# Row sums of the softmax: block sums on DVE for some tiles, turned sums on TensorE removed, two more split tiles per half

## The chip, the cores and the metric

The kernel runs on 1 core of one Trainium2 chip. The metric is the device time in microseconds of one execution; below, the median of three runs. The engines are TensorE (PE; its weight loads are shown as PEld), VectorE (DVE), ScalarE (ACT), GpSimd (POOL) and SyncE (SP), which here only issues DMAs.

## The reference, cut to what matters

A decoder layer on x [4, 256, 512] with a context of [4, 1601, 512], all in fp32:

```python
x = layernorm(x + self_attention(x))            # attention over head channels, 16 x 16 per token
x = layernorm(x + cross_attention(x, ctx))      # 32 query heads, 8 key heads of 128; keys are [ctx, x], 1857 rows
x = layernorm(x + router_mix(x))                # softmax over 64 experts, top 8

# cross attention, per batch and key head
q, k = rms_norm(x @ Wq) * qw, rms_norm(kv @ Wk) * kw
v = kv @ Wv
probs = softmax(q @ k.T / sqrt(128))            # the row sums of exp(...) are what the change is about
out = (probs @ v) @ Wo
```

## The kernel before, in words

Nearly all the time is cross attention. It is cut into 32 **units** (4 batches x 8 key heads), each of two **halves** of 2 query heads (512 columns: 2 heads x 256 queries), 64 halves in all. A half walks over 15 key **tiles** of 128 keys (the last has 65). Scores are kept transposed: keys on the partitions, the 512 query columns in the free dimension. The softmax's row sum is therefore a sum over partitions and tiles.

The whole order of work is written out by hand as numbered **steps**: step s computes the scores of tile s (`scores`), and ACT copies them into a ring of 21 rows in SBUF (`copy_scores`). DVE keeps the running maximum (`raise_max(s - 1)`); `scores(s)` waits for the maximum of tile s - 2, since there are two score banks. 18 steps later (WAIT), when the half's maximum is known, DVE shifts tile t = s - 18 (`shift`), ACT takes the exponential (`exp`), POOL does its part, and 2 steps after that PE multiplies with the values (`pv`).

Products in fp32 accuracy are done as three matmuls of split numbers (hi and lo parts, type fp32r): `three`. For the value product there are two ways. A **split** tile has P_hi from a second exponential on ACT (line 1322), P_lo from a subtraction on POOL (`lo`, line 888), and three matmuls (lines 971 to 973). A **full** tile is one fp32 product (line 1001), issued as two instructions; it needs neither. `FULL` lists the full tiles of a half per batch: 7, 5, 3 and 3 of 15. P_hi and P_lo have three buffers.

The row sums: POOL adds tile after tile into `acc` (`add`, lines 902 and 906, 14 adds per half). Then PE turns `acc` with four transposes (`turn_sums`, job "AT"), DVE reduces them to `sums` and takes the reciprocal `rinv` (lines 1726 and 1728), PE turns that again (`turn_reciprocals`, job "RT", line 1140), DVE copies it to `rrow` (line 1748), SP stores it to DRAM and loads it back spread over all partitions, and DVE multiplies the half's output `OT_n` with it (`divide`, line 1811). ACT and DVE split the result (`OT_hi`, `OT_lo`), and PE multiplies with Wo (jobs "O").

Beside this, PE does the next unit's projections: `fill(s)` gives a step's extra jobs by unit v and step c of its cycle of 30 (s = 30 v - 20 + c): "KV" (keys and values of a tile, at each even c), "Q", "QT" and "KT" (turned queries and keys), "X" (a tile of the context turned and split, via the buffers `built`), "MT" (turned maximum), "AT", "RT", "O". DVE drains a job in the step after it (`drain`), and normalises the queries at c = 13 (`normalise`, line 1675). The later tiles of the self attention (`LATER`) are products on POOL at the steps in `EVENTS`, with sums on DVE; the router of batch b runs beside a later batch. In the first batch POOL also splits the weights (`split`). Each engine's queue is in order, and each wait is on a semaphore's count.

The last unit has no next unit whose projections could run beside it: in its steps PE has scores, value products and outputs alone, and the last 20 steps have no scores either.

Of the kernel before, what the change touches and what calls it, by code (L numbers as in the profile page):

```python
# [45 lines left out]
def layer(nc, x_in, sWq, sbq, sWk, sbk, sWv, sbv, ctx_in, Wq, Wk, Wv, Wo, qw, kw, x1, y_out, Wr, rb, eb, final):  # L46
# [25 lines left out]
    FULL = [[2, 3, 6, 7, 10, 11, 14], [4, 5, 10, 11, 14], [6, 7, 14], [6, 7, 14]]  # L72
    FULL = [FULL[v // KVH] for v in range(UNITS)]
    HALF = [[j for j in range(NJ) if j not in FULL[v]] for v in range(UNITS)]
# [75 lines left out]
    def fill(s):  # L150
# [5 lines left out]
        if c % 2 == 0:  # L156
# [9 lines left out]
            12: [("RT", 2 * v - 3)],  # L166
# [9 lines left out]
            27: [("RT", 2 * v - 2), ("QT", v, 1)],  # L176
# [14 lines left out]
    def divided(s):  # L191
        return [x[1] for x in fill(s - 6) if x[0] == "RT"]
# [118 lines left out]
    def left(kind, v, at):  # L311
        return NJ * (2 * v - 3) + max(kind[v - 2][at]) + 1 if kind[v - 2][at] else 0

    with ExitStack() as ctx:
# [86 lines left out]
        built = [sb(f"built{i}", [P, 2, C, P], F32R) for i in range(2)]  # L401
# [3 lines left out]
        sums = sb("sums", [P, 2, 4])  # L405
        rinv = sb("rinv", [P, 2, 4])
        rrow = sb("rrow", [4, P])
# [113 lines left out]
        s_ri = sem("row_reciprocal")  # L521
# [76 lines left out]
        def _(e):  # L598
# [182 lines left out]
            for s in STEPS:  # L781
# [60 lines left out]
        def _(e):  # L842
# [48 lines left out]
            def add(t):  # L891
                p, j = divmod(t, NJ)
                if j == 0:
                    return
# [10 lines left out]
                e.wait_ge(s_acc, acc_no(t - 1))  # L905
# [60 lines left out]
        def _(e):  # L966
            e.wait_ge(s_id, 2)
            e.wait_ge(s_pad, 5)
# [222 lines left out]
            for s in STEPS:  # L1191
# [8 lines left out]
                for x in fill(s):  # L1200
# [12 lines left out]
                    elif x[0] == "AT":  # L1213
                        turn_sums(x[1])
# [10 lines left out]
                    elif x[0] == "RT":  # L1225
                        turn_reciprocals(x[1])
# [9 lines left out]
        def _(e):  # L1236
# [7 lines left out]
            e.wait_ge(s_pad, 5)  # L1244
# [44 lines left out]
            def copy_scores(s):  # L1289
# [11 lines left out]
                if s >= RING:  # L1301
# [6 lines left out]
                    e.wait_ge(s_acc, acc_no(t + 1 if t % NJ == 0 else t))  # L1308
# [43 lines left out]
            def high(job):  # L1352
                out = F_ps[F_AT[job] % 2][:]
                e.wait_ge(s_ff, F_AT[job] + 1)
                if job[0] == "X":
# [4 lines left out]
                    else:  # L1360
# [137 lines left out]
        def _(e):  # L1498
# [4 lines left out]
            e.wait_ge(s_pad, 5)  # L1503
# [190 lines left out]
            def drain(job):  # L1694
# [5 lines left out]
                if job[0] == "X":  # L1700
# [23 lines left out]
                elif job[0] == "AT":  # L1724
                    p = job[1]
                    e.reduce_sum(sums[:, p % 2, :], out.rearrange("p (i k) -> p i k", k=P), AX.X).then_inc(s_fr, 1)
                    e.wait_ge(s_fr, F_AT[job] + 1)
                    e.reciprocal(rinv[:, p % 2, :], sums[:, p % 2, :]).then_inc(s_ri, 1)
# [14 lines left out]
                elif job[0] == "RT":  # L1743
                    p = job[1]
                    if p:

                        e.wait_ge(s_rd, 16 * p)
                    e.tensor_copy(rrow[:], out[0:4, 0:P]).then_inc(s_fr, 1)
# [58 lines left out]

            def divide(p):
# [9 lines left out]
            for s in STEPS:  # L1818
# [69 lines left out]
```

## Time and profile before

| what | value |
|---|---|
| median of 3 runs | 2815.78 us (2813.55 to 2817.94) |
| profiled execution, own time | 2816.99 us |
| its span, first to last instruction | 2815.2 us |
| mean granted TensorE clock | 0.986 of 2.4 GHz |
| DMA | 485.6 MB, mean 173 GB/s |

Times in the profile are microseconds from the span's start, lengths of one instruction nanoseconds where marked. A PE matmul is drawn from its start to a modelled end, so that bars of neighbours overlap; DVE and ACT instructions overlap by up to some 0.1 us too. "[0.32 <-ACT ...]" behind a row is the engine's idle time before it and what ended it.

### The profile page before, as it was taken

How to read it: one execution, taken by the hardware profiler on the slowest of the kernel's cores; microseconds unless marked ns; L12 is line 12 of the kernel's file. 1: busy time of each engine (PE TensorE's matmuls, PEld its weight loads, DVE VectorE, ACT ScalarE, POOL GpSimd, SP SyncE). 2: the span in 40 equal slices, each digit the busy share in tenths (PEclk: the TensorE clock that was granted, in tenths of full speed). 3: DMA queues.
4: the chain of work that ended last, by engine and by line, in shares of the span. 5: the costliest groups of instructions: out<-in, count | busy, mean ns of one | idle time of the engine just before them, and what ended most of it. 6: DMA issues, size and time to landing. Idle time of an engine off the chain costs nothing.

```text
span 2815.2 us, 47816 instructions
## 1 busy us (share of the span) xinstructions
PE 2720.3 (97%) x14812; PEld 2220.4 (79%) x14812; DVE 2221.7 (79%) x3596; ACT 2029.4 (72%) x3945; POOL 2377.3 (84%) x2320
## 2 busy tenths in 40 slices
PE   7899999999999999999999999999999999999974
PEld 5777878777878888888888888888888888888853
DVE  5577888888778878888778887787778888788873
ACT  3577777777767777777777777777777777777771
POOL 4399999898888888878889988888898888888893
PEclk9999999999999999999999999999999999999996
DMA  6756565565555454555545455554455445344310
GB/s 234 253 184 216 193 221 193 195 213 184 183 178 200 160 177 169 182 177 196 178 147 193 167 189 174 179 184 165 156 173 173 154 158 180 124 165 150 117 42 26
DMA packets 159434, 485.64 MB, mean 173 GB/s; under 512 B 16839, under 2 KB 27849, under 8 KB 159182
## 3 DMA queue, kind: packets, MB, share of 16 engines
q1 hardware_dynamic: 157592, 481.01, 50.5%
q8 instruction: 121, 1.98, 0.3%
q10 hardware_dynamic: 1590, 1.58, 0.2%
q14 instruction: 131, 1.07, 0.1%
HBM read 403.09 MB, written 79.43 MB: 171 GB/s over the span
## 4 chain that ended last, share of the span: by engine, by line
PE 79%; POOL 9%; issue 6%; DVE 4%; ACT 2%; DMA 1%; SPq 0%; POOLq 0%; ACTq 0%; DVEq 0%
PE K_ps L971 9%; PE K_ps L973 9%; PE K_ps L972 9%; PE OT_ps L1001 7%; PE S_ps L971 6%; PE S_ps L973 6%; PE S_ps L972 6%; POOL acc L906 5%; PE OT_ps L971 5%; PE OT_ps L972 4%; PE OT_ps L973 4%; POOL P_lo L888 2%; PE F_ps L971 2%; PE F_ps L972 2%; PE F_ps L973 2%
## 5 line engine op out<-in xcount | busy, mean ns | idle before, releaser
L906 POOL TENSOR_TENSOR acc<-acc,scores 128x512 f32<-128x512 f32 (+1 forms) x832 | 1120.8, 1347 | 40.4 <-ACT scores L1323 10.1
L888 POOL TENSOR_TENSOR P_lo<-scores,P_hi 128x512 fp32r<-128x512 f32 x672 | 898.4, 1337 | 211.3 <-ACT scores L1323 210.3
L1652 DVE SCALAR_TENSOR_TENSOR running_max<-S_ps,rk,running_max 128x512 f32<-128x512 f32 (+1 forms) x896 | 669.0, 747 | 250.2 <-ACT scores L1309 247.8
L1636 DVE TENSOR_TENSOR scores<-scores,Mb_ps 128x512 f32<-128x512 f32 (+1 forms) x960 | 648.7, 676 | 134.4 <-PE Mb_ps L1127 134.3
L1309 ACT ACTIVATE scores<-S_ps,rk 128x512 f32<-128x512 f32 (+1 forms) x960 | 651.6, 679 | 139.8 <-PE S_ps L973 120.1
L1323 ACT ACTIVATE scores<-scores 128x512 f32<-128x512 f32 (+1 forms) x960 | 596.9, 622 | 59.2 <-DVE scores L1636 57.1
L1322 ACT ACTIVATE P_hi<-scores 128x512 fp32r<-128x512 f32 x672 | 423.1, 630 | 293.7 <-DVE scores L1636 213.9
L971 PE MATMUL S_ps<-QT_hi,KT_hi 128*128 128x512 f32 (+1 forms) x960 | 496.9, 518 | 14.8 <-DVE running_max L1652 13.0
L971 PE MATMUL K_ps<-Wkv_hi,kvT 128*128 128x256 f32 (+1 forms) x1664 | 470.9, 283 | 2.4 <-DVE kvT L1709 2.4
L973 PE MATMUL K_ps<-Wkv_hi,kvT 128*128 128x256 f32 (+1 forms) x1664 | 471.1, 283 | 0.0
L972 PE MATMUL K_ps<-Wkv_lo,kvT 128*128 128x256 f32 (+1 forms) x1664 | 470.3, 283 | 0.0
L973 PE MATMUL S_ps<-QT_hi,KT_lo 128*128 128x512 f32 (+1 forms) x960 | 380.6, 396 | 0.0
L972 PE MATMUL S_ps<-QT_lo,KT_hi 128*128 128x512 f32 (+1 forms) x960 | 379.3, 395 | 0.0
L971 PEld LDWEIGHTS K_ps<-Wkv_hi,kvT 128*128 128x128 f32 (+1 forms) x1664 | 310.3, 186 | 22.4 <-DVE kvT L1709 2.8
L972 PEld LDWEIGHTS K_ps<-Wkv_lo,kvT 128*128 128x128 f32 (+1 forms) x1664 | 310.3, 186 | 20.1
L971 PE MATMUL OT_ps<-P_hi,V_hi 128*128 128x512 f32 x672 | 290.3, 432 | 31.0 <-POOL P_lo L888 30.8
L973 PEld LDWEIGHTS K_ps<-Wkv_hi,kvT 128*128 128x128 f32 (+1 forms) x1664 | 310.7, 187 | 0.0
L1001 PE MATMUL OT_ps<-scores,V_full 128*128 128x512 f32 (+1 forms) x576 | 296.7, 597 | 0.0
L971 PEld LDWEIGHTS S_ps<-QT_hi,KT_hi 128*128 128x128 f32 (+1 forms) x960 | 178.1, 186 | 119.3 <-DVE running_max L1652 46.5
L972 PE MATMUL OT_ps<-P_lo,V_hi 128*128 128x512 f32 x672 | 266.6, 397 | 0.0
L973 PE MATMUL OT_ps<-P_hi,V_lo 128*128 128x512 f32 x672 | 266.0, 396 | 0.0
L972 PEld LDWEIGHTS S_ps<-QT_lo,KT_hi 128*128 128x128 f32 (+1 forms) x960 | 178.9, 186 | 92.4 <-issue 64.1
(226 smaller groups left out, 4666.8 us busy)
## 6 DMA issues: line engine op xcount, KB each, us to landing
kvT<-kvT_scratch SPq DMA_DIRECT2D x403, 512.0 KB, 3.7
Wq_hi<-weight_halves_scratch SPq DMA_DIRECT2D x48, 512.0 KB, 5.4
Wq_lo<-weight_halves_scratch SPq DMA_DIRECT2D x48, 512.0 KB, 6.6
Wo_hi<-weight_halves_scratch SPq DMA_DIRECT2D x48, 512.0 KB, 4.7
Wo_lo<-weight_halves_scratch SPq DMA_DIRECT2D x48, 512.0 KB, 5.6
kvT_scratch<-built SPq DMA_DIRECT2D x45, 512.0 KB, 4.3
rinv_spread<-rinv_scratch SPq DMA_DIRECT2D x64, 256.0 KB, 4.8
Wkv_hi<-weight_halves_scratch SPq DMA_DIRECT2D x24, 512.0 KB, 5.6
```

The source lines that it names most:

```text
L888: e.tensor_tensor(P_lo[n % PB][0:r, :], prob(t)[0:r, :], f(P_hi[n % PB][0:r, :]), ALU.subtract)\
L906: e.tensor_tensor(a[0:r, :], a[0:r, :], prob(t)[0:r, :], ALU.add).then_inc(s_acc, 1)
L971: e.matmul(out, l_hi, r_hi, start=first, stop=False)
L972: e.matmul(out, l_hi, r_lo, start=False, stop=False)
L973: return e.matmul(out, l_lo, r_hi, start=False, stop=last)
L1001: ins = e.matmul(OT_ps[:], V_full[v % 2][0:r, FULL[v].index(j), :], row[t % RING][0:r, :], start=first, stop=last)
L1309: e.activation(row[s % RING][0:r, :], S_ps[s % 2][0:r, :], ACT.Copy, scale=rk[0:r, v % 2, j:j + 1])\
L1322: e.activation(P_hi[n % PB][0:r, :], d, ACT.Exp)
L1323: e.activation(d, d, ACT.Exp).then_inc(s_p, 1)
L1636: e.tensor_tensor(d, d, Mb_ps[0:r, :], ALU.add).then_inc(s_d, 1)
L1652: e.scalar_tensor_tensor(a, src, k, a, ALU.mult, ALU.max).then_inc(s_top, 1)
```

## The change

- `SUMMED` lists three tiles of each half that POOL no longer adds. DVE sums each in blocks (`sum_tile`): a reduce that turns 32x32 blocks first, so that 128x512 becomes 128x16, the sums over the 32 partitions of each quadrant. In the last unit all 15 tiles are in `SUMMED`, and POOL adds nothing.
- When POOL's `acc` is complete, DVE takes its block sums too, and adds up the partial sums to `block_totals` [128, 16] (`sum_blocks`, in the step ahead of job "AT"). In the last unit there is no `acc`.
- "AT" is now one fp32 matmul of `block_totals` with the constant `same_in_block` [128, 32], which adds the four quadrants; the result is [16, 32]. DVE writes its reciprocal straight to `rrow`. Job "RT" is gone, and the store, the spread, `divide` and the two splits of the output come two steps earlier (`divided`).
- `FULL` loses two tiles per half: 5, 3, 1 and 1 full tiles are left. The self attention's products go by a new list, `LIGHT`.
- `built` is one buffer instead of two; ACT waits for the store of the tile before.
- In the last unit's tile of 65 keys, ACT zeroes the rows from 64 on before it copies the scores.

```diff
-    FULL = [[2, 3, 6, 7, 10, 11, 14], [4, 5, 10, 11, 14], [6, 7, 14], [6, 7, 14]]
+    FULL = [[4, 5, 10, 11, 14], [6, 7, 14], [14], [14]]
+    SUMMED = [[2, 7, 13], [2, 9, 12], [3, 7, 11], [3, 7, 11]]
+    LIGHT = [[2, 7, 11], [2, 7, 12], [], []]
...
+    SUMMED = [SUMMED[v // KVH] for v in range(UNITS - 1)] + [list(range(NJ))]
...
-            12: [("RT", 2 * v - 3)],
...
-            27: [("RT", 2 * v - 2), ("QT", v, 1)],
+            27: [("QT", v, 1)],
...
-        return [x[1] for x in fill(s - 6) if x[0] == "RT"]
+        return [x[1] for x in fill(s - 6) if x[0] == "AT"]
...
-        if j in FULL[p // 2] and j - 1 not in FULL[p // 2] and j < NJ - 1:
+        if j in LIGHT[p // 2]:
             EVENTS.append(s)
...
-        built = [sb(f"built{i}", [P, 2, C, P], F32R) for i in range(2)]
+        built = sb("built", [P, 2, C, P], F32R)
...
             def add(t):
                 p, j = divmod(t, NJ)
-                if j == 0:
+                if t not in ADD_AT:
                     return
...
-            def turn_sums(p):
-                e.wait_ge(s_acc, acc_no(NJ * p + NJ - 1))
+            def add_blocks(p):
...
+                e.wait_ge(s_bt, p + 1)
                 out = take(("AT", p))
-                for i in range(4):
-                    ins = e.transpose(out[:, i * P:(i + 1) * P], acc[p % 2][:, i * P:(i + 1) * P], ident[:])
-                ins.then_inc(s_ff, 1)
-
-            def turn_reciprocals(p):
-                e.wait_ge(s_ri, p + 1)
-                out = take(("RT", p))
-                e.transpose(out[0:4, 0:P], rinv[:, p % 2, :], ident[:]).then_inc(s_ff, 1)
+                e.matmul(out[0:16, 0:32], sums[:, p % 2, :], same[:], start=True, stop=True).then_inc(s_ff, 1)
...
+                if r < P and p in LATE:
+                    e.activation(row[s % RING][TAIL // 32 * 32:P, :], row[s % RING][TAIL // 32 * 32:P, :], ACT.Copy,
+                                 scale=0.0).then_inc(s_z, 1)
...
-                    e.reduce_sum(sums[:, p % 2, :], out.rearrange("p (i k) -> p i k", k=P), AX.X).then_inc(s_fr, 1)
-                    e.wait_ge(s_fr, F_AT[job] + 1)
-                    e.reciprocal(rinv[:, p % 2, :], sums[:, p % 2, :]).then_inc(s_ri, 1)
+                    if p:
+
+                        e.wait_ge(s_rd, 16 * p)
+                    e.reciprocal(rrow[:], out[0:16, 0:32]).then_inc(s_fr, 1)
...
+            def sum_tile(t):
+                p, j = divmod(t, NJ)
+                e.wait_ge(s_p, t + 1)
+                e.tensor_reduce(blocks_of(p)[:, SUMMED[p // 2].index(j), :], prob(t).rearrange("p (j a) -> p j a", a=32), AX.X,
+                                ALU.add, apply_transpose=True).then_inc(s_bs, 1)
+
+            def sum_blocks(p):
+                n = len(SUMMED[p // 2]) - 1
+                if p in LATE:
+                    e.wait_ge(s_bs, BLOCK_AT[NJ * p + n] + 1)
+                else:
+                    n += 1
+                    e.wait_ge(s_acc, ADD_AT[NJ * p + NJ - 1] + 1)
+                    e.tensor_reduce(blocks_of(p)[:, n, :], acc[p % 2][:].rearrange("p (j a) -> p j a", a=32), AX.X,
+                                    ALU.add, apply_transpose=True).then_inc(s_bs, 1)
+                    e.wait_ge(s_bs, BLOCK_AT["acc", p] + 1)
...
+                e.reduce_sum(sums[:, p % 2, :], blocks_of(p)[:, 0:n + 1, :].rearrange("p k j -> p j k"), AX.X)\
+                    .then_inc(s_bt, 1)
...
+                if 0 <= s - WAIT - 1 < NS and summed_tile(s - WAIT - 1):
+                    sum_tile(s - WAIT - 1)
+                for x in fill(s + 1):
+                    if x[0] == "AT":
+                        sum_blocks(x[1])
                 for p in divided(s - 2):
                     OT_low(p)
                 for p in divided(s):
```

## Rows read from the trace of the kernel before

**Rows 1.** The page, part 1: busy time, share of the span, instructions.
```profile
PE 2720.3 (97%) x14812; PEld 2220.4 (79%) x14812; DVE 2221.7 (79%) x3596; ACT 2029.4 (72%) x3945; POOL 2377.3 (84%) x2320
```

**Rows 2.** Busy time by stretch: length, PE, PEld, DVE, ACT, POOL, granted clock, DMA.
```profile
90.00:2678.00 2588.00, 2564.45 (x14206) 2117.53 (x14206) 2101.88 (x3392) 1944.83 (x3784) 2256.03 (x2210) 1.00 0.53 178
...
2075.00:2720.00 645.00, 633.07 (x3472) 521.56 (x3472) 540.23 (x891) 484.29 (x953) 560.44 (x555) 0.99 0.44 144
2720.00:2816.00 96.00, 50.71 (x148) 30.44 (x146) 40.96 (x79) 23.66 (x45) 47.94 (x38) 0.71 0.10 33
```

**Rows 3.** Waits of PE, 90 to 2678 us; last line 2678 to 2769 us.
```profile
PE S_ps L971 <- DVE running_max L1652: 13.0, 13, 1.8
PE OT_ps L971 <- POOL P_lo L888: 6.7, 10, 1.4
...
PE OT_ps L971 <- POOL P_lo L888: 24.1, 23, 1.9
```

**Rows 4.** Timeline of PE, 1732 to 1737 us: start, length, engine, line.
```profile
1732.84 1.02 PE L1001 MATMUL OT_ps<-scores,V_full 128*128 128x512 f32 x2
...
1733.30 0.80 PE L971 MATMUL S_ps<-QT_hi,KT_hi 128*128 128x512 f32 x1
...
1733.93 0.39 PE L972 MATMUL S_ps<-QT_lo,KT_hi 128*128 128x512 f32 x1
1734.16 0.39 PE L973 MATMUL S_ps<-QT_hi,KT_lo 128*128 128x512 f32 x1
...
1735.83 0.40 PE L971 MATMUL OT_ps<-P_hi,V_hi 128*128 128x512 f32 x1
...
1736.53 0.39 PE L971 MATMUL S_ps<-QT_hi,KT_hi 128*65 128x512 f32 x1
```

**Rows 5.** Timeline of PE around an AT job.
```profile
1714.51 0.60 PE L1134 MATMUL F_ps<-ident,acc 128*128 128x128 f32 x4
...
1715.18 0.39 PE L972 MATMUL OT_ps<-P_lo,V_hi 128*128 128x512 f32 x1
```

**Rows 6.** Small PE operations: the "RT" group, and router logits in the timeline.
```profile
L1140 PE MATMUL F_ps<-ident,rinv 128*4 128x128 f32 x64 | 17.5, 274 | 0.0
...
2224.50 1.90 PE L1161 MATMUL F_ps<-self_qkv,w_stage 128*128 128x64 f32 x16
```

**Rows 7.** Groups of DVE instructions: busy us, mean ns, idle before and releasers.
```profile
L1660 DVE TENSOR_REDUCE ss_k<-sq 128x4 f32<-128x512 f32 x96 | 65.3, 680 | 30.1 <-ACT sq L1419 29.9
...
L1726 DVE TENSOR_REDUCE sums<-F_ps 128x4 f32<-128x512 f32 x64 | 43.7, 682 | 13.2 <-PE F_ps L1134 12.7
...
L1728 DVE RECIPROCAL rinv<-sums 128x4 f32<-128x4 f32 x64 | 11.4, 179 | 2.2
...
L1748 DVE COPY rrow<-F_ps 4x128 f32<-4x128 f32 x64 | 17.4, 272 | 2.4 <-PE F_ps L1140 1.6
...
L1811 DVE TENSOR_TENSOR OT_n<-OT_n,rinv_spread 128x512 f32<-128x512 f32 x64 | 76.3, 1192 | 7.0 <-DMA rinv_spread<-rinv_scratch 7.0
```

**Rows 8.** Timeline of DVE, steps 13 to 17 of a unit's cycle.
```profile
1721.27 3.37 DVE L1675 TENSOR_TENSOR natq<-natq,rq 128x512 f32<-128x512 f32 x2
...
1730.51 0.67 DVE L1636 TENSOR_TENSOR scores<-scores,Mb_ps 128x512 f32<-128x512 f32 x1
1731.49 0.75 DVE L1652 SCALAR_TENSOR_TENSOR running_max<-S_ps,rk,running_max 128x512 f32<-128x512 f32 x1 [0.32 <-ACT scores L1309]
```

**Rows 9.** 2699 to 2769 us: busy time of the engines, and POOL's groups.
```profile
2699.00:2769.00 70.00, 49.56 (x164) 30.29 (x164) 40.07 (x57) 38.74 (x70) 68.51 (x54) 0.87 0.12 38
...
L906 POOL TENSOR_TENSOR acc<-acc,scores 128x512 f32<-128x512 f32 (+1 forms) x28 | 36.7, 1311 | 1.0
L888 POOL TENSOR_TENSOR P_lo<-scores,P_hi 128x512 fp32r<-128x512 f32 x24 | 31.5, 1316 | 0.0
```

**Rows 10.** Timeline of the end, after the last value product.
```profile
2769.07 1.06 PE L1134 MATMUL F_ps<-ident,acc 128*128 128x128 f32 x4
...
2772.61 0.27 DVE L1748 COPY rrow<-F_ps 4x128 f32<-4x128 f32 x1
```

More of the change, by code:

```diff
@@ L71, in layer @@
     TOP = 8
-    FULL = [[2, 3, 6, 7, 10, 11, 14], [4, 5, 10, 11, 14], [6, 7, 14], [6, 7, 14]]
+    FULL = [[4, 5, 10, 11, 14], [6, 7, 14], [14], [14]]
+    SUMMED = [[2, 7, 13], [2, 9, 12], [3, 7, 11], [3, 7, 11]]
+    LIGHT = [[2, 7, 11], [2, 7, 12], [], []]
     FULL = [FULL[v // KVH] for v in range(UNITS)]
+    SUMMED = [SUMMED[v // KVH] for v in range(UNITS - 1)] + [list(range(NJ))]
+    LIGHT = [LIGHT[v // KVH] for v in range(UNITS)]
+    ADDED = [NJ * p + j for p in range(HALVES) for j in range(1, NJ) if j not in SUMMED[p // 2]]
+    LATE = [p for p in range(HALVES) if len(SUMMED[p // 2]) == NJ]
+    ADD_AT = {t: n for n, t in enumerate(ADDED)}
     HALF = [[j for j in range(NJ) if j not in FULL[v]] for v in range(UNITS)]
@@ L312, in left @@
         return NJ * (2 * v - 3) + max(kind[v - 2][at]) + 1 if kind[v - 2][at] else 0
+    BLOCKS = []
+    for s in STEPS:
+        if 0 <= s - WAIT - 1 < NS and summed_tile(s - WAIT - 1):
+            BLOCKS.append(s - WAIT - 1)
+        BLOCKS += [("acc", x[1]) for x in fill(s + 1) if x[0] == "AT" and x[1] not in LATE]
+    BLOCK_AT = {x: n for n, x in enumerate(BLOCKS)}
     with ExitStack() as ctx:
@@ L404, in layer @@
         nm = sb("nm", [P, 2, 4])
-        sums = sb("sums", [P, 2, 4])
-        rinv = sb("rinv", [P, 2, 4])
-        rrow = sb("rrow", [4, P])
+        blocks = sb("block_sums", [P, 2, max(map(len, SUMMED[:-1])) + 1, 16])
+        sums = sb("block_totals", [P, 2, 16])
+        same = sb("same_in_block", [P, 32])
+        rrow = sb("rrow", [16, 32])
         rb_all = sb("rinv_spread", [P, QW])
@@ L520, in layer @@
         s_mb = sem("negated_max_spread")
-        s_ri = sem("row_reciprocal")
+        s_same = sem("same_in_block")
+        s_z = sem("last_tile_rows_zeroed")
+        s_bs = sem("block_sums")
+        s_bt = sem("block_totals")
         s_rd = sem("row_reciprocals_stored")
@@ L703, in store_tile @@
                 k = x_no(b, n)
-                src = tile[k % 3] if b == 0 else built[k % 2]
+                src = tile[k % 3] if b == 0 else built
                 e.wait_ge(s_fr, F_AT["X", b, n] + 1)
@@ L847, in _ @@
             for i in range(2):
-                e.memset(f(built[i][:]), 0.0).then_inc(s_pad, 1)
                 e.memset(nat[i][:], 0.0).then_inc(s_pad, 1)
+            e.memset(f(built[:]), 0.0).then_inc(s_pad, 1)
             e.memset(eps[:], EPS).then_inc(s_pad, 1)
@@ L1213, in _ @@
                     elif x[0] == "AT":
-                        turn_sums(x[1])
+                        add_blocks(x[1])
                     elif x[0] == "FR":
@@ L1502, in _ @@
             e.wait_ge(s_w, 1)
-            e.wait_ge(s_pad, 5)
+            e.wait_ge(s_pad, 4)
+            e.wait_ge(s_id, 2)
+            e.reduce_sum(same[:], ident[:].rearrange("p (i a) -> p a i", a=32), AX.X).then_inc(s_same, 1)
             e.wait_ge(sa_w, 32)
@@ L1706, in drain @@
                         k = x_no(b, n)
-                        to = tile[k % 3] if b == 0 else built[k % 2]
+                        to = tile[k % 3] if b == 0 else built
                         hi, dst = to[:, 0, :, 0:r], to[:, 1, :, 0:r]
@@ L1742, in drain @@
                         .then_inc(s_fr, 1)
[L1743 to L1748, printed above, removed]
                 else:
```

45 lines of the change are left out of this document (28 added, 17 removed).

## The prediction, made before the changed kernel was run

> **What bounds the kernel now.** The first view to read is the page's list of busy shares: TensorE (PE) 97%, POOL 84%, DVE 79%, ACT 72% [rows 1]. One average says little here, so the next is the table by stretch: from 90 to 2678 us PE is busy 2564 of 2588 us at full clock, POOL 2256, DVE 2102. The last 96 us are another regime, with PE busy 51 us at a mean clock of 0.71 [rows 2]. The waits of PE agree: in the long middle it waits 13.0 us for DVE's running maximum and 6.7 us for POOL's P_lo; between 2678 and 2769 us it waits 24.1 us for P_lo alone [rows 3].
>
> So there are two kernels in one. In the middle PE sets the pace, and only fewer PE microseconds, or a new stall of PE, move the end. In the last unit no projections of a next unit fill PE, and each tile needs up to two POOL passes; POOL sets the pace there.
>
> Matmul bars overlap, so PE's costs are read as distances between starts, not as lengths. A split tile of the value product (three matmuls) runs from 1735.83 to the next start at 1736.53: 0.70 us. A full fp32 tile starts at 1732.84; the score matmul behind it is drawn early but its successor starts at 1733.93, and the usual distance to that is 0.23 (1733.93 to 1734.16), so the full tile takes 1733.93 - 0.23 - 1732.84 = 0.86 us [rows 4]. Four transposes of the sums start at 1714.51, the second matmul behind them at 1715.18: 1715.18 - 0.23 - 1714.51 = 0.44 us, 0.11 each [rows 5].
>
> A rule of the Trainium skill ("Perfetto Trace Analysis", section on the most-contended engine) says that matmul busy time is a bad measure of headroom and that weight-load busy time is the better one. By that, PE would have 18% to spare in the middle (2118 of 2588 us of loads [rows 2]) and the PE term below would be worth nothing. The rows with starts 0.23 us apart without a gap speak against it, so I keep it as a rival.
>
> **PE, the middle.** There are 62 halves (of 64) ahead of the last unit. In each, two tiles go from full to split: 2 x (0.86 - 0.70) = 0.32 us less. The four transposes of `turn_sums` (0.44) and the one of `turn_reciprocals` (0.11; 64 of these in the trace, [rows 6]) go: 0.55 us less. What comes instead is one fp32 matmul of 16 columns of weights by 32 moving columns, which the trace lacks. A fp32 product is issued as two instructions, as in the full tile ("x2" for one tile); the nearest row is 16 instructions of 64 columns in 1.90 us, 0.11 or 0.12 each [rows 6]. So it costs at most 0.23 and at least about 0.05; I take 0.20, near the upper end because the small matmul also has to load its weights. Net per half: 0.32 + 0.55 - 0.20 = 0.67 us, times 62 = **41.5 us less** (39.7 to 51 by the bounds).
>
> **POOL, the middle.** Each half loses three adds and gains two subtractions, all of 1.32 us [rows 9]: 1.3 us less per half. POOL isn't on the path except for the 6.7 us of P_lo waits [rows 3]. They arise where weight splits and self-attention products queue ahead of `lo`, in the first batch mostly, and the new split tiles put P_lo work there too. I take 3 us less (0 to 7).
>
> **DVE, the middle.** Per half it gains three block sums of tiles, one of `acc`, and a sum of 4 x 16 partials; it loses the reduce of the turned sums (682 ns), a reciprocal of 4 (179 ns) and the copy of the reciprocals (272 ns), and gets a reciprocal of 16x32 from PSUM (taken as the copy, 0.27) [rows 7]. No row has a transposing reduce. The nearest is the plain reduce of 128x512 from SBUF, 680 ns, and that from PSUM, 682 ns [rows 7]. Starts of neighbouring 128x512 operations are 0.60 to 0.66 apart [rows 8], so one costs 0.6 in a queue. Lower bound 0.6; upper bound twice it, 1.3, if four-byte blocks pass the transposer at half rate. I take 0.68, since input, output count and engine are those of that row. Net 4 x 0.6 + 0.2 + 0.27 - 1.13 = +1.7 us per half. From 2075 to 2720 us DVE is busy 540 of 645 us [rows 2]; 15 halves make it 566 of about 635, 89%. That is no bound on average, so the place matters.
>
> For this one price there is only a page: the Trainium skill ("Vector Engine (DVE) Microarchitecture Reference", 3.8) says the 32x32 transposer sustains one element per cycle per lane. By it the block sum stays at the plain reduce's 0.68 and the sum at the time forecast here; no run here shows it yet.
>
> The place is step 16 of each cycle. Just before, DVE is late: `normalise` at step 13 took 3.4 us at 1721.27 [rows 8]. PE's scores need the running maximum of two steps ago. At step 17 DVE did the shift at 1730.51, right behind the work of step 16, then had 0.32 us idle before the maximum at 1731.49 [rows 8]; that ends at 1732.24, and PE wants it at 1733.30 [rows 4]: 1.06 us to spare, plus the 0.32 idle. Now the division of `OT_n` (mean 1.19 us, since POOL works beside it, [rows 7]) moves from step 18 to 16, with the block sum of tile 7 (0.6) in three of four batches. That is 1.2 to 1.8 us more against 1.4 of slack, and PE comes 0.3 us earlier. I expect a PE stall of 0.6 us per unit (0 to 1.5), times 31 = **18 us more** (0 to 45). The other new places lie in light steps: the sum of `acc` at steps 9 and 24 comes after the maximum that PE needs, and the former `sums` and `rrow` free 1.1 us behind it.
>
> ACT gets 128 `P_hi` more and one V_hi copy per unit. It is busy 1945 of 2588 us with 3784 instructions [rows 2], 0.5 us each; even at 0.7 the 160 more make 112 us, 80% in all, beside PE's work. If this cover went, the same maximum at step 17 would be late, which is in the range above. The SP queue has the same store and spread, two steps earlier; the reciprocals leave from [16, 32] instead of [4, 128], with the same 2 KB. The single `built` buffer makes ACT wait for the store of the previous tile, issued 4 or more steps (10 us) earlier; nothing.
>
> **The end.** From 2699 to 2769 us POOL is busy 68.5 of 70 us with 30 adds and 24 subtractions [rows 9]. After the change it has 28 subtractions, 28 x 1.32 = 37 us. Next in line is DVE: 40 us now [rows 9], plus 30 block sums at 0.6, less the removed 2.3: 56 us. ACT has 39 us [rows 9] and four more exponentials. So DVE sets the pace, at 56 instead of 70: **14 us less** (10 to 22). Behind the last value product, four transposes at 2769.07, the reduce, a transpose behind an output product, and the copy up to 2772.88 [rows 10] shrink to one small matmul and a reciprocal, some 0.8 us: **3 us less**. The DMA round trip of the reciprocals behind it stays.
>
> **Sum.** The profiled execution has 2817.0 us around its span of 2815.2, 1.2 us above the median of the three, so both are one number for this purpose. -41.5 - 3 + 18 - 14 - 3 = -43.5: **2773 us** (ratio 0.985). DVE's first reduce for `same` adds 0.3 us in the opening and one memset less on POOL takes about as much away.
>
> **Rivals.**
> 1. *The transposing reduce is slow, and DVE becomes the bound: slower.* At 1.3 us DVE has 4 x 0.65 = 2.6 us more per half, 4.3 in all: 606 of 635 us in the stretch from 2075, 95%. About half of 62 x 2.6 = 161 would show as stalls, +80; the end gains nothing on DVE (56 + 18 = 74 us), so +14 too. 2773 + 94 = 2867. Below some 1.0 us per block sum the change still gains. For it: only that the form is unknown. Chance 0.10.
> 2. *Step 16 costs more.* The division takes the 1.7 us that each of the two multiplications of `normalise` took, the same kind of instruction [rows 8], and the block sum falls in front of it: 1.5 us per unit. 2773 + 28 = 2801. Chance 0.15.
> 3. *DVE waits for POOL's last add.* `sum_blocks` now sits on DVE, two steps behind the scheduled add of tile 14, and queues the next shift and maximum behind it, on which ACT and PE wait. At 0.5 us per half: +31, 2804. For it: PE's AT job comes a step later than DVE's sum does now. Against it: of PE's waits in the middle none of any size names `acc` [rows 3], and POOL has less to do. Chance 0.07.
> 4. *PE isn't the bound in the middle* (the rule named above; here the ring of maximum, scores and exponentials would set the pace). Then -17 at the end and +0 to 18: 2800 to 2818, say 2812. Chance 0.05.
> 5. *The slack holds at step 16,* and the P_lo waits go: 2750. Chance 0.13.
>
> The likeliest has 0.50. A change under 0.2% (5.6 us) can't be told from none here; 2811.4 is the line. Faster: 0.50 + 0.15 + 0.07 + 0.13 and less than half of 4, 0.86, from which I take 0.02 for what isn't listed: 0.84. Same: 0.05. Slower: 0.11. The range from 2745 to 2812 leaves out rival 1 and a little at the low end. The likeliest's own is 2758 to 2790.
>
> **What would show it.** Right: a PE busy time some 40 us lower with the same clock; `block_sums` rows near 0.68 us; POOL some 115 us less busy; the last unit at under 2 us per tile with DVE near full; a wait of PE for the running maximum that grows from 13 us to some 30, at steps 17 and 18 of the cycle. Wrong: `block_sums` above 1 us; a wait of DVE on `acc`; a full tile that costs PE no more than a split one where POOL is late.

## The result, and the profile after

The changed kernel takes **2827.18 us** (median; 2826.48 to 2834.98), against 2815.78: ratio 1.0049, 95% interval 1.0033 to 1.0065. It is slower by 0.5%; forecast was 2773, and the time lies outside the range.

Part 1 of the page of the changed kernel, beside [rows 1]:

```profile
PE 2695.0 (95%) x14748; PEld 2219.5 (79%) x14748; DVE 2375.8 (84%) x3811; ACT 2084.9 (74%) x4107; POOL 2269.0 (80%) x2233
```

PE is busy for 25 us less (some 40 were forecast) and POOL for 108 less (115), and the span is still 9.5 us longer (2824.7). The table says where. It is made from the starts of the second score product (`S_ps<-QT_lo,KT_hi`; the first is often drawn early) of steps 10, 220, 460, 700 and 940 in the timeline of PE, which are the borders of the batches; in the kernel before they are 112.1, 692.9, 1356.6, 2008.8 and 2677.7 us, after 110.4, 724.2, 1388.6, 2040.7 and 2704.8.

| stretch | before | after | difference |
|---|---|---|---|
| up to step 10 | 112.1 | 110.4 | -1.7 |
| batch 0 (7 units) | 580.8 | 613.8 | **+33.0** |
| batch 1 (8) | 663.7 | 664.3 | +0.7 |
| batch 2 (8) | 652.1 | 652.2 | 0.0 |
| batch 3 (8) | 669.0 | 664.1 | -4.9 |
| last unit's end | 137.5 | 119.9 | **-17.6** |

So the end gave what was forecast (-17), and the middle was to give 26.5 us and took 28.8. The run e10 below has no stretches, since its profiled execution was a disturbed one of 5345 us. The waits of PE in the changed kernel, batch by batch (us in total, times, longest); the kernel before has 13.0 us for the maximum in all of them [rows 3]:

```profile
PE S_ps L992 <- DVE running_max L1677: 34.2, 15, 5.2
PE OT_ps L992 <- POOL P_lo L909: 3.5, 6, 1.4
...
PE S_ps L992 <- DVE running_max L1677: 9.3, 10, 1.6
...
PE S_ps L992 <- DVE running_max L1677: 7.7, 7, 1.1
...
PE S_ps L992 <- DVE running_max L1677: 5.9, 8, 1.1
```

There are few long waits in batch 0 and many of one microsecond later. The groups of DVE show which instructions became costly. First the new ones, over the whole execution:

```profile
L1831 DVE TRANSPOSE_TENSOR_REDUCE block_sums<-scores 128x16 f32<-128x512 f32 x186 | 129.9, 698 | 0.0
L1841 DVE TRANSPOSE_TENSOR_REDUCE block_sums<-acc 128x16 f32<-128x512 f32 x62 | 43.6, 703 | 0.0
L1847 DVE TENSOR_REDUCE block_totals<-block_sums 128x16 f32<-128x64 f32 x62 | 16.4, 265 | 2.1
L1754 DVE RECIPROCAL rrow<-F_ps 16x32 f32<-16x32 f32 x64 | 21.4, 335 | 2.5 <-PE F_ps L1156 2.5
```

They cost about what was taken for them (0.68 was forecast for a block sum, 0.2 for the sum of partials, 0.27 for the reciprocal). What grew are old instructions. The same two groups in batch 0, the kernel before first and the changed kernel second:

```profile
L1675 DVE TENSOR_TENSOR natq<-natq,rq 128x512 f32<-128x512 f32 x14 | 18.1, 1330 | 0.0
L1811 DVE TENSOR_TENSOR OT_n<-OT_n,rinv_spread 128x512 f32<-128x512 f32 x12 | 12.4, 1037 | 0.0
```
```profile
L1700 DVE TENSOR_TENSOR natq<-natq,rq 128x512 f32<-128x512 f32 x14 | 30.5, 2216 | 2.0 <-POOL rq L951 2.0
L1853 DVE TENSOR_TENSOR OT_n<-OT_n,rinv_spread 128x512 f32<-128x512 f32 x12 | 22.3, 1862 | 0.0
```

Neither multiplication was changed, and 26 of them take 22 us more. The timeline of unit 5's steps 13 to 17 in the changed kernel shows beside what: first DVE, then POOL, then PE.

```profile
492.01 4.57 DVE L1700 TENSOR_TENSOR natq<-natq,rq 128x512 f32<-128x512 f32 x2 [0.43 <-POOL rq L951]
...
503.58 0.70 DVE L1831 TRANSPOSE_TENSOR_REDUCE block_sums<-scores 128x16 f32<-128x512 f32 x1
504.20 2.54 DVE L1853 TENSOR_TENSOR OT_n<-OT_n,rinv_spread 128x512 f32<-128x512 f32 x1
506.67 1.74 DVE L1622 TENSOR_TENSOR self_x<-self_x,self_small 128x512 f32<-128x512 f32 x1
508.33 0.67 DVE L1661 TENSOR_TENSOR scores<-scores,Mb_ps 128x512 f32<-128x512 f32 x1
508.93 0.74 DVE L1677 SCALAR_TENSOR_TENSOR running_max<-S_ps,rk,running_max 128x512 f32<-128x512 f32 x1
```
```profile
491.78 0.20 POOL L951 TENSOR_TENSOR rq<-nrm_q 128x8 f32<-128x8 f32 x1
491.94 2.40 POOL L966 TENSOR_TENSOR Wq_lo<-w_stage,Wq_hi 128x1024 fp32r<-128x1024 f32 x1
...
503.82 2.38 POOL L966 TENSOR_TENSOR Wo_lo<-w_stage,Wo_hi 128x1024 fp32r<-128x1024 f32 x1 [0.81 <-ACT Wo_hi L1472]
```
```profile
509.73 0.65 PE L992 MATMUL S_ps<-QT_hi,KT_hi 128*128 128x512 f32 x1 [4.32 <-DVE running_max L1677]
```

The division starts at 504.20, POOL's split of Wo_lo runs from 503.82 to 506.20, and the division ends at 506.74: it lasts until the pass is over, and ends 0.54 us behind it. `natq` does the same: its wait for `rq` ends with the very instruction that stands ahead of POOL's split of Wq_lo, so it starts in step with 2.4 us of POOL work (the first of the two multiplications takes 2.87 us here). When POOL rests, the division takes 0.69 us; here it is in the tail of the same execution:

```profile
2789.47 0.69 DVE L1853 TENSOR_TENSOR OT_n<-OT_n,rinv_spread 128x512 f32<-128x512 f32 x1 [1.79 <-DMA rinv_spread<-rinv_scratch]
```

The Trainium skill has this rule ("GPSIMD Engine Reference", section 8, Key points): GpSimd shares its SBUF interfaces with VectorE, with contention for DVE instructions that have two SBUF inputs. The trace agrees: the block sum at 503.58, with one input, kept its 0.70 us.

How many passes such an instruction waits for isn't fixed. Another one is the subtraction that makes `OT_lo`, also of two SBUF tiles. Here it is at step 3 of unit 10, the kernel of run e2 below first (DVE, then POOL) and the changed kernel second:

```profile
896.12 5.10 DVE L1857 TENSOR_TENSOR OT_lo<-OT_n,OT_hi 128x512 fp32r<-128x512 f32 x1
895.61 1.30 POOL L927 TENSOR_TENSOR acc<-acc,scores 128x512 f32<-128x512 f32 x1
896.87 2.55 POOL L909 TENSOR_TENSOR P_lo<-scores,P_hi 128x512 fp32r<-128x512 f32 x2
899.37 1.30 POOL L927 TENSOR_TENSOR acc<-acc,scores 128x512 f32<-128x512 f32 x1
```
```profile
903.28 1.35 DVE L1857 TENSOR_TENSOR OT_lo<-OT_n,OT_hi 128x512 fp32r<-128x512 f32 x1
```

The code of this batch is the same in both kernels, and in both the instruction starts 0.51 us into the add (902.77 in the changed kernel). In one it ends behind that pass, and the next POOL pass takes 1.76 instead of 1.30 us; in the other it ends behind the fourth, after 5.10 us. Why isn't known. There are also cases in which POOL alone is longer: the division at 553.19 took 0.65 us, and P_lo, which started at 553.24, took 1.76.

In batch 2 there are no weight splits. The same steps in unit 20, DVE and then PE:

```profile
1761.61 0.70 DVE L1831 TRANSPOSE_TENSOR_REDUCE block_sums<-scores 128x16 f32<-128x512 f32 x1
1762.23 1.53 DVE L1853 TENSOR_TENSOR OT_n<-OT_n,rinv_spread 128x512 f32<-128x512 f32 x1
1763.69 0.68 DVE L1661 TENSOR_TENSOR scores<-scores,Mb_ps 128x512 f32<-128x512 f32 x1
1764.29 0.74 DVE L1677 SCALAR_TENSOR_TENSOR running_max<-S_ps,rk,running_max 128x512 f32<-128x512 f32 x1
```
```profile
1765.08 0.50 PE L992 MATMUL S_ps<-QT_hi,KT_hi 128*128 128x512 f32 x1 [1.10 <-DVE running_max L1677]
```

From the block sum to the next shift it is 1763.69 - 1761.61 = 2.08 us that the kernel before doesn't have at this place, and PE waits 1.10. That is the step on which the forecast turned. PE waits at step 18 of the cycle in 7 of the 8 units of batch 2 (7.7 us), in all 7 of batch 0 (21.6), and in fewer of batch 1 (4.5) and 3 (2.3); in the kernel before these waits come to 2.2 us in all four.

The third part is the clock. Batch 0 before and after (length, PE, PEld, DVE, ACT, POOL, granted clock, DMA), and ten microseconds before and behind the wait of 4.3 us:

```profile
112.00:693.00 581.00, 569.40 (x3098) 458.76 (x3098) 467.95 (x751) 432.69 (x818) 522.61 (x485) 1.00 0.60 207
```
```profile
112.00:726.00 614.00, 576.09 (x3087) 467.80 (x3086) 522.78 (x792) 445.53 (x857) 509.09 (x473) 0.97 0.58 196
...
500.00:510.00 10.00, 5.68 (x31) 4.35 (x30) 9.68 (x12) 6.71 (x14) 8.89 (x8) 1.00 0.55 188
510.00:520.00 10.00, 10.00 (x52) 8.41 (x52) 8.53 (x16) 8.89 (x17) 8.99 (x10) 0.83 0.48 170
```

After the wait of 4.3 us PE is busy throughout from 510 to 520, at a mean granted clock of 0.83: a part of the stretch at 1.2 instead of 2.4 GHz. PE's idle time in batch 0 grew from 11.6 to 37.9 us (+26.3), and its busy time by 6.7 us although it has some 8 us less work (7 units at 1.16, measured below). So some 15 us of batch 0 are work at the lower clock, the rest waits. The trace's own clock says the same: it was at 1.2 GHz for 31 us of batch 0, which cost half of that, and for none in the kernel before.

### The profile page after: what moved, and what is told of

Read it like the earlier page. It is cut to its first block, busy times and chain, and to the rows that moved or that the text cites. A ratio compares the mean times of both kernels' runs of the same rounds, so it can differ in the third digit from the quotient of the medians.

```text
span 2824.7 us, 47987 instructions
## 1 busy us (share of the span) xinstructions
PE 2695.0 (95%) x14748; PEld 2219.5 (79%) x14748; DVE 2375.8 (84%) x3811; ACT 2084.9 (74%) x4107; POOL 2269.0 (80%) x2233
## 4 chain that ended last, share of the span: by engine, by line
PE 72%; DVE 10%; issue 7%; POOL 6%; ACT 3%; DMA 1%; SPq 0%; POOLq 0%; ACTq 0%; DVEq 0%
PE K_ps L992 8%; PE K_ps L994 8%; PE K_ps L993 8%; PE S_ps L992 6%; PE S_ps L994 6%; PE S_ps L993 6%; PE OT_ps L992 5%; PE OT_ps L993 5%; PE OT_ps L994 5%; PE OT_ps L1022 4%; POOL P_lo L909 3%; DVE running_max L1677 2%; DVE scores L1661 2%; POOL acc L927 2%; PE F_ps L992 1%
## 5 line engine op out<-in xcount | busy, mean ns | idle before, releaser
L909 POOL TENSOR_TENSOR P_lo<-scores,P_hi 128x512 fp32r<-128x512 f32 x800 | 1063.3, 1331 | 334.1 <-ACT scores L1344 329.4
L927 POOL TENSOR_TENSOR acc<-acc,scores 128x512 f32<-128x512 f32 x620 | 837.6, 1351 | 29.3 <-ACT scores L1344 11.5
L1343 ACT ACTIVATE P_hi<-scores 128x512 fp32r<-128x512 f32 x800 | 504.7, 631 | 410.3 <-DVE scores L1661 296.0
L992 PE MATMUL S_ps<-QT_hi,KT_hi 128*128 128x512 f32 (+1 forms) x960 | 449.0, 468 | 64.4 <-DVE running_max L1677 61.7
L992 PE MATMUL OT_ps<-P_hi,V_hi 128*128 128x512 f32 x800 | 342.5, 428 | 13.7 <-POOL P_lo L909 13.6
L993 PE MATMUL OT_ps<-P_lo,V_hi 128*128 128x512 f32 x800 | 317.3, 397 | 0.0
L994 PE MATMUL OT_ps<-P_hi,V_lo 128*128 128x512 f32 x800 | 316.2, 395 | 0.0
L994 PEld LDWEIGHTS S_ps<-QT_hi,KT_lo 128*128 128x128 f32 (+1 forms) x960 | 178.1, 185 | 44.8 <-issue 0.2
```

The lines of the kernel that those rows point to most:

```text
L909: e.tensor_tensor(P_lo[n % PB][0:r, :], prob(t)[0:r, :], f(P_hi[n % PB][0:r, :]), ALU.subtract)\
L927: e.tensor_tensor(a[0:r, :], a[0:r, :], prob(t)[0:r, :], ALU.add).then_inc(s_acc, 1)
L992: e.matmul(out, l_hi, r_hi, start=first, stop=False)
L993: e.matmul(out, l_hi, r_lo, start=False, stop=False)
L994: return e.matmul(out, l_lo, r_hi, start=False, stop=last)
L1343: e.activation(P_hi[n % PB][0:r, :], d, ACT.Exp)
```

## The experiments

All are edits of the changed kernel, timed in turn with the kernel before. The columns are the difference of each stretch to the kernel before, from the same score products as above and from one profiled execution each. The stretch up to step 10 is left out; it differs by -3.6 to +1.1 us.

| run | us | ratio to before, interval | batch 0 | 1 | 2 | 3 | end |
|---|---|---|---|---|---|---|---|
| changed kernel | 2827.18 | 1.0049 [1.0033, 1.0065] | +33.0 | +0.7 | 0.0 | -4.9 | -17.6 |
| e1_divide_late | 2825.57 | 1.0037 [1.0024, 1.0050] | +33.0 | -0.6 | -2.7 | -3.8 | -15.3 |
| e2_no_sum_at_16 | 2815.23 | 0.9997 [0.9987, 1.0007] | +28.7 | +8.9 | -6.3 | -9.1 | -18.2 |
| e3_both | 2802.57 | 0.9953 [0.9938, 0.9968] | +21.5 | -3.0 | -9.3 | -7.2 | -15.7 |
| e4_light_old | 2828.69 | 1.0046 [1.0031, 1.0061] | +28.2 | +6.9 | +0.2 | -4.8 | -16.3 |
| e5_full_old | 2815.03 | 0.9991 [0.9982, 1.0000] | +9.1 | +18.6 | -1.8 | -5.2 | -21.2 |
| e6_b0_full_2_3 | 2789.41 | 0.9899 [0.9884, 0.9913] | +9.1 | -1.9 | -9.1 | -7.1 | -15.1 |
| e12_e6_divide_early | 2807.42 | 0.9962 [0.9948, 0.9976] | +13.6 | +7.7 | -6.4 | -9.0 | -15.7 |
| e7_acc_and_end | 2795.45 | 0.9916 [0.9899, 0.9933] | -1.7 | -2.5 | -1.7 | +0.6 | -14.7 |
| e9_wq_split_14 | 2810.12 | 0.9967 [0.9955, 0.9979] | +21.9 | -1.3 | -9.1 | -7.3 | -11.1 |
| e10_b0_light | 2780.70 | 0.9868 [0.9853, 0.9883] | | | | | |
| e11_b0_early_tile | **2776.82** | 0.9863 [0.9849, 0.9878] | -5.0 | -2.2 | -9.2 | -7.4 | -14.0 |

Batch 1 has the same code in the changed kernel, e2 and e4 (and, but for batch 0 ahead of it, in e12), and came out at +0.7, +8.9, +6.9 and +7.7. The traces show why: e2, e4 and e12 have two, one and two `OT_lo` there that took 4.5 to 5.1 us, as the one above, and the changed kernel has none. Such a difference in batch 1 alone is therefore no effect of an edit's own work.

**e1_divide_late.** The division goes back to step 18.

```diff
-        return [x[1] for x in fill(s - 6) if x[0] == "AT"]
+        return [x[1] for x in fill(s - 8) if x[0] == "AT"]
```

> The changed kernel with the division, OT_hi and OT_lo back at the steps they had before (18, 19, 20 and 3, 4, 5 of the cycle); all else as changed. Theory A (the move of the division to step 16, where POOL's weight split and DVE's backlog meet, costs most of the loss): PE's wait for the maximum at step 18 falls from 22 us (first batch) and 8 us (third) to a few; 2827 falls by 25 to 40 us, to 2787 to 2802. Rival B (DVE is simply too full, wherever the work lies): the stall moves to steps 19 to 21 and the time stays within 10 us, 2817 to 2827.

Measured: 2825.57, next to nothing, as rival B said. The division fell from 1.86 to 1.46 us in batch 0 and PE's waits at step 18 from 21.6 to 13.4, but waits for P_lo at step 19 rose from 1.4 to 6.4, and the batch is as long as before the edit. In batch 2 a wait of 0.4 us at step 20 took the place of that of 1.1 at step 18 (2.7 us less).

**e2_no_sum_at_16.** The block sum of tile 7 goes to tile 8.

```diff
-    SUMMED = [[2, 7, 13], [2, 9, 12], [3, 7, 11], [3, 7, 11]]
+    SUMMED = [[2, 8, 13], [2, 9, 12], [3, 8, 11], [3, 8, 11]]
```

> The changed kernel with tile 8 in place of tile 7 in SUMMED (batches 0, 2, 3), so that the block sum comes one step after step 16; division stays at 16. Theory A with the block sum as a part: it is worth its own 0.6 us in 24 units, 10 to 15 us, 2812 to 2817. Rival C (the block sum ahead of the division is the main cost, since it pushes the division behind POOL's next pass): 25 us or more, below 2802. Rival B: nothing, 2822 to 2828.

Measured: 2815.23, in theory A's range. Batch 2 gives 6.3 us back, batch 0 4.3 and batch 3 4.2 against the changed kernel; batch 1 takes 8.2 more, with the two long `OT_lo`.

**e3_both.** Both edits.

> Both edits: division late and tile 8 for tile 7. Theory A: the PE work saved (35 us in the middle) and the end (17 us) come through, less the stalls of before: 2772 to 2785. Rival B: 2810 or more.

Measured: 2802.57, between what theory A and rival B said. Alone, the edits give 1.6 and 12.0 us, together 24.6. Against the sum of both alone, batch 2 is 0.3 us shorter and batch 3 0.8 longer, so there the edits simply add up. The surplus is in batch 0 (7.2 us) and in batch 1 (10.6), which has no block sum at step 16; most of the latter is that e3 has none of the long `OT_lo` of e2. That the place of a division only counts without a block sum in front of it isn't shown. Batch 2 now has no wait of PE at all:

```profile
1375.00:2017.00 642.00, 642.00 (x3644) 544.04 (x3643) 541.96 (x862) 516.73 (x1025) 547.13 (x555) 1.00 0.54 179
```

PE is busy 642.00 of 642.00 us, and the batch is 9.3 us shorter than before, 9.3 / 8 = **1.16 us per unit**. This is the PE term of the change by itself. Batch 0 is left at +21.5, with its `natq` still at 2.2 us and its division at 1.2:

```profile
L1853 DVE TENSOR_TENSOR OT_n<-OT_n,rinv_spread 128x512 f32<-128x512 f32 x12 | 14.2, 1182 | 0.0
```

**e4_light_old and e5_full_old.** Is batch 0 slow for the places of the self attention's products, or for POOL's P_lo of the new split tiles?

```diff
-    LIGHT = [[2, 7, 11], [2, 7, 12], [], []]
+    LIGHT = [[2, 6, 10], [2, 7, 12], [], []]
```

> The changed kernel with the self attention's products of the first batch at the tiles of before (LIGHT 2, 6, 10 for 2, 7, 11), so that their residual add (1.7 us on DVE) no longer lies in step 16. Only batch 0 can move. If that step's sum of work is what counts: 5 to 12 us less, 2815 to 2822. If the weight split beside the division is: nothing, 2825 to 2830.

```diff
-    FULL = [[4, 5, 10, 11, 14], [6, 7, 14], [14], [14]]
+    FULL = [[2, 3, 6, 7, 10, 11, 14], [4, 5, 10, 11, 14], [6, 7, 14], [6, 7, 14]]
```

> The changed kernel with the FULL lists of before: no additional split tiles, division still at step 16. PE loses the 0.18 us that each of two tiles per half saved (22 us in the middle). Theory A2 (in the first batch the new split tiles 2 and 3 put a POOL pass ahead of the queries' factors, so that the normalisation meets the weight split, 2.9 us instead of 1.3): batch 0 gets back 15 us or more, so that the whole ends at 2815 to 2830. Rival (split tiles have no part in the stalls): 2847 or so.

Measured: 2828.69 and 2815.03. The old places of the products alone give 4.8 us in batch 0, which a long `OT_lo` in batch 1 takes back. The old full tiles take batch 0 from +33.0 to +9.1 and its `natq` to 1433 ns, though PE has more work there, so it is mostly the new P_lo work that holds batch 0 up. Batch 1 becomes 18 us worse in e5: PE waits 18.8 us there instead of 12.2, the lower clock costs 6.8 us instead of nothing, and the two more full tiles per half cost 8 x 4 x 0.17 = 5.4.

**e6_b0_full_2_3.** e3_both, with tiles 2 and 3 full again in batch 0, 4 and 5 split: the same PE work but for position.

```diff
-    FULL = [[4, 5, 10, 11, 14], [6, 7, 14], [14], [14]]
+    FULL = [[2, 3, 10, 11, 14], [6, 7, 14], [14], [14]]
```

> The kernel with division late and tile 8 for 7 (2802.6 us), and in the first batch the full tiles 2, 3, 10, 11, 14 in place of 4, 5, 10, 11, 14. Theory A2: the first length of the normalisation in batch 0 falls from 2.9 to 1.3 to 1.8 us, and the stall at step 18 with it: 8 to 14 us less, 2789 to 2795. Rival (the block sums ahead of it are the cause): no more than 3 us.

Measured: 2789.41, as theory A2 said, 13.2 us less than e3_both, 12.4 of them in batch 0. As many tiles are split as in e3, so it is their place that counts. The group of `natq` in batch 0:

```profile
L1700 DVE TENSOR_TENSOR natq<-natq,rq 128x512 f32<-128x512 f32 x14 | 19.5, 1431 | 0.0
```

Without the P_lo of tiles 2 and 3 ahead of it, POOL is earlier with `rq` (no wait for it is left), and `natq` mostly starts some 1.95 us into the pass of the split instead of with it. PE's waits in batch 0 fall from 30.0 to 20.0 us; of what is left, 10.6 are for P_lo (7.2 in e3).

**e12_e6_divide_early.** e6 with the division at step 16, no block sum in front.

> The 2789 us kernel with the division at step 16 as in the changed kernel. With the late division alone the changed kernel gained 2 us, with both edits 25; so the division's place matters only where the block sum is not in the same step. If that is so: 6 to 14 us more than 2789, 2795 to 2803. If the place never mattered and the 25 us came from tile 8 alone: 2787 to 2792.

Measured: 2807.42, 18 us more than e6, above the expected 2803. Of these 9.6 us are in batch 1 and 4.5 in batch 0 (and 4.5 up to step 10, where neither kernel differs); batch 3 is 1.9 us shorter. In batch 0 `natq` stays at 1.43 us and the division goes back to its long time:

```profile
L1853 DVE TENSOR_TENSOR OT_n<-OT_n,rinv_spread 128x512 f32<-128x512 f32 x12 | 22.1, 1839 | 0.0
```

Five DVE instructions with two SBUF inputs take 3.5 to 5.1 us in this run: two divisions in batch 0, one division and two `OT_lo` in batch 1. The changed kernel, e3, e5, e6, e7, e9 and e11 have none over 3 us in the profiled execution. So part of what this edit cost is which of the two engines went first, and not the step by itself.

Over all runs, `natq` of batch 0 is at 2.21 to 2.22 us with tiles 2 and 3 split (changed kernel, e1 to e4) and at 1.43 to 1.54 with them full (e5, e6, e7, e11, e12); with the split of Wq at another step (e9, below) it is at 1.74. The division goes by no such rule: at step 16 it took 1.86 us in the changed kernel, 1.21 in e2, 1.42 in e4, 1.48 in e5 and 1.84 in e12, at step 18 1.46 in e1, 1.18 in e3 and 1.23 in e6. What counts for it is the moment at which it meets POOL's pass, not the step that it is written in.

**e7_acc_and_end.** Only the block sum of `acc`, the new "AT" and the last unit's block sums; POOL adds all tiles of the other halves, `FULL` as before, division at step 18.

> Only the block sum of acc (with the one small matmul and without job RT) and the last unit's 15 block sums; no tile of the middle is summed by DVE, FULL and the products' tiles as before, division late. Single built buffer. If the turned sums' removal is worth 0.45 us per unit on PE (14 us), the end 17 us, and DVE has room for the sum of acc: 2783 to 2790. If DVE's 0.9 us more at steps 9 and 24 stall PE: 2798 or more.

Measured: 2795.45, between the two expectations. No batch is slower by more than 0.6 us and the end gives 14.7. These parts carry next to no stall; what the middle adds to them (split tiles and block sums of tiles) is what the stalls come from.

**e9_wq_split_14.** e3_both with the split of Wq at step 14 instead of 11, behind `natq`.

```diff
-            chunk = {5: ("Wkv", v + 1, 0), 11: ("Wq", v + 1, 0), ...
+            chunk = {5: ("Wkv", v + 1, 0), 14: ("Wq", v + 1, 0), ...
```

> The kernel with division late and tile 8 for 7 (2802.6 us), and POOL's (and ACT's) split of the first half of Wq at step 14 instead of 11, behind the normalisation. Theory (a DVE operation with two inputs in SBUF waits out the POOL operation that is running): the first of the two multiplications in units 1 to 6 takes at most 1.8 us instead of 2.9, the stall at step 18 falls by 1 us each, 5 to 8 us in all, unless two weight splits in a row make P_lo late (up to +10). If the length has another cause, it stays at 2.9.

Measured: 2810.12, 7.5 us more than e3_both, where 5 to 8 less were expected. The first multiplication of `natq` fell from 2.87 to 1.77 us, as the theory said, and batch 0 stays at +21.9: PE's waits for P_lo rose from 7.2 to 12.1 us there, the exception that the expectation had named. A shorter `natq` alone gives no time back. 4.6 of the 7.5 us are in the end, which has no split; that isn't explained.

**e10_b0_light and e11_b0_early_tile.** Both are edits of e6 (division late, tile 8 for 7). Batch 0 keeps POOL's order nearly as before: six full tiles, one block sum. e11 also builds the context's tile 2 two steps earlier, for the single buffer `built`.

```diff
+    FULL = [[2, 3, 6, 7, 10, 11], [6, 7, 14], [14], [14]]
+    SUMMED = [[13], [2, 9, 12], [3, 8, 11], [3, 8, 11]]
+    LIGHT = [[2, 6, 10], [2, 7, 12], [], []]
...
-        3: [("KV", 0, 13)],
+        3: [("KV", 0, 13), ("X", 1, 2)],
...
-        5: [("X", 1, 2)],
```

> The 2789 us kernel (division late, tile 8 for 7, full tiles 2 and 3 kept in batch 0) with batch 0 nearly as before: full tiles 2, 3, 6, 7, 10, 11, only tile 13 summed by DVE, products at 2, 6, 10. In the kernel with only acc and the end changed, batch 0 took 1.7 us less than before; here it took 9.1 more. If the remaining loss of batch 0 comes from its block sums and P_lo beside the weight splits: 7 to 11 us less, 2778 to 2783. If it comes from the single built buffer or the sum of acc: within 3 us of 2789.

> The same with the first tile of the second batch built at step 3 instead of 5, so that the store of the only built buffer has landed before the next one at step 9. ACT waited 5.1 us for that store in the changed kernel and PE 2.9 us behind it. If that wait is what costs: 2 to 3 us less than the run beside it; if another wait takes its place: the same.

Measured: 2780.70 and **2776.82**, ratio 0.9863, the fastest version: 1.4% below the kernel before, 50 us below the changed one. Batch 0 of e11, windows and waits of PE:

```profile
109.00:685.00 576.00, 564.21 (x3072) 455.62 (x3071) 478.46 (x766) 440.63 (x840) 521.91 (x485) 1.00 0.61 208
```
```profile
PE S_ps L991 <- DVE running_max L1676: 2.7, 3, 1.8
```

The clock is back at 1.00, and PE waits 2.7 us for the maximum instead of 34.2. The early tile answers to this row of the changed kernel, one wait of ACT at the start of unit 1:

```profile
115.41 0.60 ACT L1395 ACTIVATE built<-F_ps 128x512 fp32r<-128x512 f32 x1 [5.06 <-DMA kvT_scratch<-built]
```

The difference of e10 and e11 is within their intervals.

## Why the prediction was wrong

**The step that failed** is the DVE stall at step 16, "0.6 us per unit (0 to 1.5), times 31 = 18 us more", the sum's only term for new stalls. By e3_both the middle is worth 31 x 1.16 = 36.0 us less when nothing stalls (measured in batch 2, carried over to the others); it came out 28.8 more, so stalls and what they cost in clock are 64.8 us, against 15 in the forecast (18 less the 3 of P_lo): 2.1 us per unit. They are 41.1 in batch 0 (33.0 + 7 x 1.16), and 10.0, 9.3 and 4.4 in batches 1 to 3. The traces of before and after split them:

- PE's waits at step 18, which the term was about, grew from 2.2 to 36.1 us, 34 instead of 18: 21 of them in batch 0, 3 us per unit. In batch 2 it was 0.9 per unit, because the sum of 1.2 and 0.6 us was too low: 0.62 for the block sum and 1.46 for the division from start to start. e3_both shows it, since batch 2 has no wait left there.
- PE's other waits, which the forecast had at nothing new or less, grew by 11 us (all waits from 21.9 to 67.2).
- The lower clock cost 13.7 us more: 15.4 more in batch 0, 1.7 less in batch 3. It was in no term.
- The remaining 6 us of the 64.8 are open.

By experiment, moving both things from step 16 takes back all of the 9.3 us in batch 2, 2.3 of 4.4 in batch 3, 3.7 of 10.0 in batch 1 and 11.5 of 41.1 in batch 0. So the mechanism of the forecast is shown for batch 2; in batch 1, with no block sum at that step, most of the loss is elsewhere, and what causes it stays open. In batch 0 I priced the division by its mean of the kernel before, 1.19 us, though I named POOL as the reason for that mean; a mean over places says nothing of a new place beside a pass of 2.4 us. And I costed the new P_lo passes only as waits of PE for P_lo. Those stayed as they were in the changed kernel; what the passes of tiles 2 and 3 did was to delay `rq` and bring `natq` in step with the split of Wq. Taking them away is worth 12.4 us by e6; how much of that is `natq` alone isn't shown, since e9 shortened it and gained nothing. The other 17.2 us of batch 0 go, but for 3.1, with the six full tiles and the one block sum of e11; which of these does it wasn't tried apart.

**The other terms.** PE: 1.16 us per unit instead of 1.34, so -36 instead of -41.5. The rows (PE, changed kernel):

```profile
1783.94 1.02 PE L1022 MATMUL OT_ps<-scores,V_full 65*128 65x512 f32 x2
...
1785.04 0.39 PE L993 MATMUL S_ps<-QT_lo,KT_hi 128*128 128x512 f32 x1
1785.27 0.39 PE L994 MATMUL S_ps<-QT_hi,KT_lo 128*128 128x512 f32 x1
1785.59 0.23 PE L1156 MATMUL F_ps<-same_in_block,block_totals 128*16 128x32 f32 x2
1785.75 0.66 PE L1123 MATMUL F_ps<-ident,nat 128*128 128x128 f32 x4
```

A full tile takes 1785.04 - 0.23 - 1783.94 = 0.87, as read before. The small matmul takes 1785.75 - 1785.27 - 0.23 = 0.25 here, not 0.20, above the upper bound of 0.23; 62 times 0.05 is 3 of the missing 5.5 us, the rest stays open. P_lo: no gain instead of 3. The last unit: from step 940 to the sum's matmul behind the last value product it is 2783.75 - 2704.8 = 79.0 instead of 2769.07 - 2677.7 = 91.4 us [rows 10], 12.4 less against 14. DVE is near full there and POOL is not:

```profile
2725.00:2783.00 58.00, 45.66 (x158) 30.14 (x157) 52.54 (x86) 41.52 (x73) 38.40 (x30) 0.88 0.16 46
```

Behind it, 5.2 us less against 3. That the two sum up to the forecast is in part luck: the lower clock cost 28.9 us from step 940 on in the kernel before and 22.4 in the changed one, and the forecast had no term for it. `built` was costed at nothing; ACT waited 5.1 us once, and e10 and e11, which differ in this wait, can't be told apart by their times.

**The rivals.** 1 fell: the block sum takes 0.698 us. 2 came nearest: the division took 1.5 us in batch 2 (1.7 in the rival) and 2.5 beside a weight split in batch 0, and PE's waits at step 18 grew by 34 us (46 in the rival). Its 2801 lacks the other waits and the clock, as my sum does. 3 fell: DVE never waited on `acc` (0.0 before L1841). 4 fell by e3_both: PE is busy 642.00 of 642.00 us, the distances between starts give 4 x 0.17 + 2 x (0.55 - 0.25) = 1.28 us less work per unit, and the time fell by 1.16. Weight loads are busy for 544 of these 642 us, so the rule of the Trainium skill that the prediction names ("Perfetto Trace Analysis", "Identifying the Most-Contended Engine") would have given nothing; the measurement decides against it here. 5 fell: the waits at step 18 grew.

## What to carry to other kernels

Price an instruction that is moved by what runs beside it at its new place, not by its mean: here one multiplication took 0.69, 1.53 or 2.54 us, and a subtraction of two SBUF tiles took 1.35 or 5.10 at one and the same place. When work is taken off one engine and other work put on it, ask which of its results now come at another moment, and what starts with them. And when two edits are tried apart and together, look in which stretch the surplus lies before calling it their joint effect: here most of it lay in a batch that one of them didn't touch.

## What the runs showed of the hardware

- A DVE multiplication of two SBUF tiles of 128x512 takes 0.69 us with POOL idle, and 2.54 us beside a POOL pass of 2.38 us: it waits the pass out, and ends 0.54 us behind it. It can also be passed over again: a subtraction of two SBUF tiles, started 0.51 us into a pass of 1.3 us, took 1.35 us in one kernel and 5.10, behind four passes in a row, in another. And at one place (553.19) it kept its 0.65 us and the POOL pass that started 0.05 us later took 1.76 instead of 1.30. A reduce with one input stayed at 0.70.
- A reduce that turns 32x32 blocks costs what a plain one costs, 698 against 680 ns for 128x512 in fp32.
- Waits of PE cost more than their length: the mean granted clock was 0.83 in the ten microseconds behind one of 4.3 us, and in batch 0 some 15 us of lower clock came on top of 26 of waiting.
